# The row of the maxima as four products of 32 rows for two score tiles, and the head's weights' copy and statistics in another order

## The reference

```python
h = group_norm(x)                                   # 32 groups
q, k, v = h Wq + bq, h Wk + bk, h Wv + bv           # 64 channels each
attn = softmax((q . k) * 64 ** -0.5, axis=-1)       # 1024 x 1024 per image
x = x + (attn v) Wo + bo
```

## Time and profile before

| | |
|---|---|
| median of 3 runs | 186.11 us |
| profiled execution | 186.48 us |
| its span on the core | 184.0 us |
| PE busy | 174.6 us (95%), 1223 products |
| DVE busy | 138.3 us (75%) |
| ACT busy | 100.4 us (55%) |
| POOL busy | 121.8 us (66%) |

### The profile page before, as it was taken

One profiled execution on the slowest core, in us unless ns is written; L12 is line 12 of the kernel. 1 busy time (PEld: TensorE's weight loads), 2 busy tenths in 40 slices (PEclk: granted clock), 3 DMA queues, 4 the chain that ended last, 5 costly groups with the idle time before them and its releaser, 6 DMA issues.

```text
span 184.0 us, 3303 instructions
## 1 busy us (share of the span) xinstructions
PE 174.6 (95%) x1223; PEld 93.5 (51%) x1223; DVE 138.3 (75%) x208; ACT 100.4 (55%) x137; POOL 121.8 (66%) x81
## 2 busy tenths in 40 slices
PE   7778899999999999999999999999999999999993
PEld 4435545555525644455535645555535555456661
DVE  2799987779887687859875787769875588386763
ACT  3479367606656376436666476527656554466500
POOL 5265017996799929996699949996799939705000
PEclk9999999999999999999999999999999999999999
DMA  5544100500016000420025000500025100110111
GB/s 154 189 100 98 34 2 0 114 4 2 0 34 142 2 0 14 102 60 0 0 54 122 0 4 20 136 18 0 5 59 115 61 0 21 37 61 7 50 57 57
DMA packets 7103, 8.89 MB, mean 48 GB/s; under 512 B 1656, under 2 KB 4144, under 8 KB 7088
## 3 DMA queue, kind: packets, MB, share of 16 engines
q1 hardware_dynamic: 6080, 7.84, 16.9%
q10 hardware_dynamic: 1008, 0.86, 1.6%
HBM read 1.58 MB, written 1.05 MB: 14 GB/s over the span
## 4 chain that ended last, share of the span: by engine, by line
PE 82%; DVE 13%; DMA 1%; issue 1%; POOL 0%; ACT 0%; DVEq 0%; POOLq 0%
PE ps_attn L887 27%; PE ps_max L817 9%; DVE part_max L588 8%; PE ps_scores L855 8%; PE ps_scores L871 7%; PE ps_scores L857 7%; PE ps_scores L859 7%; PE ps_scores L796 3%; PE ps_misc L804 2%; PE ps_attn L894 2%; PE ps_misc L900 2%; DMA xs<-x_dram 1%; PE ps_misc L894 1%; DVE quarter_rden L628 1%; PE ps_misc L831 1%
## 5 line engine op out<-in xcount | busy, mean ns | idle before, releaser
L313 POOL TENSOR_TENSOR prob_sum<-prob_sum,probs 128x1024 f32<-128x1024 f32 x41 | 97.5, 2377 | 29.0 <-ACT probs L441 16.8
L588 DVE TENSOR_REDUCE part_max<-ps_max 128x2 f32<-128x1024 f32 x60 | 73.4, 1224 | 26.3 <-PE ps_max L818 25.8
L441 ACT ACTIVATE probs<-ps_scores 128x1024 f32<-128x1024 f32 x62 | 61.0, 1025 | 46.1 <-PE ps_scores L872 45.4
L887 PE MATMUL ps_attn<-probs,vals 128*64 128x512 f32 x224 | 54.5, 605 | 0.0
L887 PEld LDWEIGHTS ps_attn<-probs,vals 128*64 128x64 f32 x224 | 13.5, 136 | 27.8 <-issue 19.2
L871 PE MATMUL ps_scores<-q_row,ones_r 64*128 64x512 f32 x62 | 24.5, 396 | 0.5 <-ACT q_row L423 0.5
L872 PE MATMUL ps_scores<-q_row,ones_r 64*128 64x512 f32 x62 | 24.6, 396 | 0.0
L817 PE MATMUL ps_max<-back,front 64*128 64x512 f32 x31 | 13.9, 449 | 2.3 <-DVE part_max L588 1.4
L817 PE MATMUL ps_max<-cross,front 64*128 64x512 f32 x29 | 14.6, 505 | 0.3 <-DVE part_max L588 0.3
L818 PE MATMUL ps_max<-cross,back 64*128 64x512 f32 x29 | 14.6, 505 | 0.0
L818 PE MATMUL ps_max<-front,back 64*128 64x512 f32 x31 | 14.0, 450 | 0.0
(11 more groups left out here) (157 smaller groups left out, 365.7 us busy)
## 6 DMA issues: line engine op xcount, KB each, us to landing
cross<-front SPq DMA_DIRECT2D x16, 128.0 KB, 2.3
cross<-back SPq DMA_DIRECT2D x16, 128.0 KB, 2.3
rden<-quarter_rden SPq DMA_DIRECT2D x44, 32.0 KB, 1.8
xs<-x_dram SPq DMA_DIRECT2D x4, 256.0 KB, 4.6
out_dram<-xs SPq DMA_DIRECT2D x3, 256.0 KB, 2.0
rden<-quarter_rden ACTq DMA_DIRECT2D x12, 32.0 KB, 1.9
q_row<-max_rows SPq DMA_DIRECT2D x14, 2.0 KB
layer<-layers_dram SPq DMA_DIRECT2D x1, 194.5 KB, 2.7
```

Of the source, the lines that this page charges most:

```text
L313: pool.tensor_tensor(total[:, :], total[:, :], probs[t][:, :], ALU.add).then_inc(added, 1)
L441: act.activation(probs[t][:, :], scores_buffer(u, t)[:, :], ACT.Exp, scale=SCALE).then_inc(exp_done, 1)
L588: dve.tensor_reduce(part_max[u % 2][:, at:at + 2 * JS + 1:2 * JS], ps[:, :].rearrange("p (g n) -> p g n", g=2), AX.X, ALU.max, negate=True ...
L887: mm = pe.matmul(ps_attn[half * C:(half + 1) * C, :], v, probs[t][:, cols], start=(t == 0), stop=(t == TILES - 1))
```

## The change

Three things change. For pairs of score tiles a new function `rows_of_pair` adds the row of the maxima to both tiles with four products of 32 rows, on partitions 0 to 31, 32 to 63, 64 to 95 and 96 to 127: left and right half of two tiles. For this SP writes the maxima on four partitions (0, 32, 64, 96), with four transfers a unit in place of two from unit 2 on. Where it is called with `first=True`, its products open the two tiles and `scores_main` closes them; with `first=False` (tiles 0 and 1) they close both. It is used in the loop for all four pairs and in the last unit for tiles (0, 1), (3, 4) and (6, 7). Where `scores_row` stays (units 0 and 1, tiles 2 and 5 of the last unit), it takes its ones from a new matrix `first_r`, which is one on partitions 0 and 64 and zero elsewhere, so that a row that is there twice counts once.

In the head, ACT copies the weights of layer 0 (`copy_setup(0)`), and DVE's `setup` goes. DVE's first step of the statistics of image 1 moves ahead of `affine(0)`.

```diff
             def place_rows(u):
...
-                for n in range(2):
-                    row = q_row[u % 2][n * C:n * C + 1, :].bitcast(F32).rearrange("p (t n) -> p t n", t=JS)
+                for q in (0, 2, 1, 3)[:2 if u == 1 else 4]:
+                    row = q_row[u % 2][q * QUARTER:q * QUARTER + 1, :].bitcast(F32).rearrange("p (t n) -> p t n", t=JS)
+                    n = q // 2
                     sp.dma_start(row, max_rows[n * JS:(n + 1) * JS, :].bitcast(F32)).then_inc(row_in[u % 2], 16)
...
             pool.memset(q_row[1][:, :].bitcast(F32), 0.0).then_inc(rows_zero, 1)
+            pool.memset(first_r[:, :].bitcast(F32), 0.0).then_inc(first_zero, 1)
+            pool.wait_ge(first_zero, 1)
+            for n in range(2):
+                pool.memset(first_r[n * C:n * C + 1, :].bitcast(F32), 1.0).then_inc(first_r_set, 1)
+            pool.wait_ge(first_r_set, 2)
             root(1)
...
             set_back(0)
+            copy_setup(0)
             apply_norm_first()
...
             own_stats(0)
             share_stats(0)
             join_stats(0)
+            own_stats(1)
             affine(0)
             apply_norm_first()
-            setup(0)
-            own_stats(1)
             share_stats(1)
...
-            def scores_main(u, t):
-                front_u, back_u, cross_u = front[u % RING], back[u % RING], cross[u % RING]
+            def scores_ready(u, t):
                 if t == 0:
...
+            def scores_main(u, t, row_first=False):
+                front_u, back_u, cross_u = front[u % RING], back[u % RING], cross[u % RING]
+                if not row_first or t == 0:
+                    scores_ready(u, t)
...
+                if row_first:
+                    mm.then_inc(scores_mm, 1)
...
-                pe.matmul(left, ones_r[top, :], row[top, :], start=False, stop=True)
-                pe.matmul(right, ones_r[low, :], row[low, :], start=False, stop=True).then_inc(scores_mm, 1)
+                pe.matmul(left, first_r[top, :], row[top, :], start=False, stop=True)
+                pe.matmul(right, first_r[low, :], row[low, :], start=False, stop=True).then_inc(scores_mm, 1)
+
+            def rows_of_pair(u, t, first=True):
+                row = q_row[u % 2]
+                if t == 0:
+                    pe.wait_ge(row_in[u % 2], last_row(u))
+                for i in range(2):
+                    if first and (t or i):
+                        scores_ready(u, t + i)
+                    elif first and u:
+                        pe.wait_ge(exp_done, TILES * u - 1)
+                    ps = scores_buffer(u, t + i)
+                    for n, cols in enumerate(halves()):
+                        lanes = quarter(2 * n + i)
+                        mm = pe.matmul(ps[:, cols], ones_r[lanes, :], row[lanes, :], start=first, stop=not first)
+                if not first:
+                    mm.then_inc(scores_mm, 2)
...
                 next_max(2)
-                scores(w, 0)
-                scores(w, 1)
+                scores_main(w, 0)
+                scores_main(w, 1)
+                rows_of_pair(w, 0, False)
                 next_max(3)
...
                 next_max(4)
-                scores(w, 2)
-                scores(w, 3)
+                rows_of_pair(w, 2)
+                scores_main(w, 2, True)
+                scores_main(w, 3, True)
                 next_max(5)
...
                 values(w, 0)
                 if prep:
-                    scores(w, 4)
+                    rows_of_pair(w, 4)
+                    scores_main(w, 4, True)
                     next_max(6)
-                    scores(w, 5)
+                    scores_main(w, 5, True)
                     pe.wait_ge(exp_done, TILES * w + 5)
                     project(w + 2)
...
-                scores(w, 6)
-                scores(w, 7)
+                rows_of_pair(w, 6)
+                scores_main(w, 6, True)
+                scores_main(w, 7, True)
                 next_max(9)
```

More of the change, by code:

```diff
@@ L71, in attention_pair @@
         ones_r = sb("ones_r", [P, P], F32R)
+        first_r = sb("first_r", [P, P], F32R)
         minus_half = sb("minus_half", [P, 1])
@@ L113, in attention_pair @@
         ones_r_set = sem("ones_r_set")
+        first_zero = sem("first_zero")
+        first_r_set = sem("first_r_set")
         half_set = sem("half_set")
@@ L122, in attention_pair @@
         setup_mm = sem("setup_mm")
-        setup_done = sem("setup_done")
         wvo_set = sem("wvo_set")
@@ L183, in last_row @@
         def last_row(unit):
-            return 32 * (unit // 2) if unit % 2 == 0 else 32 * (unit // 2 + 1)
+            return 64 * (unit // 2) if unit % 2 == 0 else 64 * (unit // 2) + 32
         def low_count(later, head, unit):
@@ L410, in bias_x @@
             def bias_x(u):
[L411 to L414, removed]
+                act.wait_ge(wvo_set, u // B + 1)
                 act.wait_ge(h_ready, u + 1)
@@ L628, in reciprocal @@
                 dve.reciprocal(quarter_rden[:, cols], sums).then_inc(quarter_done, 1)
[L630 to L638, removed]
             def pair_tail(u):
@@ L854, in scores_main @@
                 left, right = ps[:, HI], ps[:, LO]
-                pe.matmul(left, key_top[top, hi], front_u[top, HI], start=True, stop=False)
-                pe.matmul(right, key_low[low, hi], back_u[low, HI], start=True, stop=False)
+                pe.matmul(left, key_top[top, hi], front_u[top, HI], start=not row_first, stop=False)
+                pe.matmul(right, key_low[low, hi], back_u[low, HI], start=not row_first, stop=False)
                 pe.matmul(left, key_top[top, hi], front_u[top, LO], start=False, stop=False)
                 pe.matmul(right, key_low[low, hi], back_u[low, LO], start=False, stop=False)
-                pe.matmul(left, key_top[top, lo], front_u[top, HI], start=False, stop=False)
-                pe.matmul(right, key_low[low, lo], back_u[low, HI], start=False, stop=False)
+                pe.matmul(left, key_top[top, lo], front_u[top, HI], start=False, stop=row_first)
+                mm = pe.matmul(right, key_low[low, lo], back_u[low, HI], start=False, stop=row_first)
+                if row_first:
+                    mm.then_inc(scores_mm, 1)
             def scores_row(u, t):
@@ L949, in _ @@
             project(0)
-            pe.wait_ge(setup_done, 1)
+            pe.wait_ge(wvo_set, 1)
             project_v(0)
@@ L981, in _ @@
             scores_main(0, 0)
-            pe.wait_ge(wvo_set, 1)
+            pe.wait_ge(wvo_set, 2)
             pe.wait_ge(max_joined, 1)
@@ L985, in _ @@
             pe.wait_ge(ones_r_set, 1)
+            pe.wait_ge(first_r_set, 2)
             scores_row(0, 0)
@@ L1102, in _ @@
                     project_v(w + 2)
-            scores(LAST, 0)
-            scores(LAST, 1)
+            scores_main(LAST, 0)
+            scores_main(LAST, 1)
+            rows_of_pair(LAST, 0, False)
             scores(LAST, 2)
@@ L1110, in _ @@
             denominators(LAST - 1)
-            scores(LAST, 3)
-            scores(LAST, 4)
+            rows_of_pair(LAST, 3)
+            scores_main(LAST, 3, True)
+            scores_main(LAST, 4, True)
             scores(LAST, 5)
@@ L1116, in _ @@
             values(LAST, 1)
-            scores(LAST, 6)
-            scores(LAST, 7)
+            rows_of_pair(LAST, 6)
+            scores_main(LAST, 6, True)
+            scores_main(LAST, 7, True)
             values(LAST, 2)
```

## The result

| | before | after |
|---|---|---|
| median | 186.04 us (185.86 to 186.34, 4 runs) | 189.9 us (188.72 to 190.46, 4 runs) |
| ratio, 95% interval | | 1.0183 [1.0147, 1.022] |
| profiled execution, span | 186.48, 184.0 us | 188.72, 186.8 us |
| a loop unit (mean of three) | 20.47 us | 21.24 us |

The kernel became slower, as forecast (189.0). The measured median lies 0.1 us above the upper end of the range (184.0 to 189.8); the ratio answers to 189.4 (186.04 x 1.0183).

The account below looks back on a forecast made before the run. PE was taken to bound the kernel (82% of the wait chain). Shape changes and late tiles less saved slots gave +3.3 us, the head -0.44, so +2.9 on the 186.11 median: 189.0 us, range 184.0 to 189.8.

Parts of the forecast that it names:

- The price of a change: On PE, each switch between 64*128 and 32*128 was taken to cost 0.19 us, between bounds of nothing and 0.19.
- The waits in a steady unit: Units w = 2 to 5: late exponentials delay DVE's sum and the projection; +0.37, +0.56 less overlap and +0.15, together +0.71 us each.
- pair (6,7): Last tile pair of a steady unit: two changes of shape against one saved slot, +0.15 us.
- Changes less slots: In w = 6, where DVE has no statistics, changes alone were counted: 7 x 0.19 - 4 x 0.23 = +0.41 us.
- w = 6 and the last unit: Final two units, counted by shape changes less saved slots alone: +0.41 us and +0.07 us.
- The head: Before the loop, DVE's first projection shift at 8.85 instead of 9.29: -0.44 us, bounds -0.87 and nothing.
- The upper bound: Top of the forecast range, 189.8 us, from the head's bounds and 0.02 of doubt on each of 39 changes.
- the sum: Row products +3.3 us over all units; with the head's -0.44, +2.9 us for the whole change.
- Free mixing: Rival: all 39 added shape changes on PE cost nothing, so saved slots win; -2.15 us, 184.0 us, chance 0.28.
- stop without load: Rival: 32-row weights are loaded ahead on PE, a change costs only 0.08; no change, 186.1 us, chance 0.08.
- two by two: Rival: PE's four 32-row products run in twos, each pair loses its slot; 5.3 us more, 194.3 us, chance 0.06.

Follow-up runs that it names:

- rows of 32 at the old places: Kernel before with each row of the maxima multiplied as two products of 32 rows instead of 64, same places and order: 207.22 us.
- Tiles 0 and 1 put back alone: The pairs alone, but with the first two tiles of each unit in the old form: 187.85 us, ratio 1.0085.
- pairs of 64 rows: The pairs alone, same order and waits, but each pair's row as four products of 64 rows in two slots: 188.65 us, ratio 1.0119.
- the pairs alone: Kernel before with only the row products of the change, the head left as before: 190.12 us, ratio 1.0227.
- the copy alone: Kernel before with only the weights' copy moved to ACT, statistics of image 1 in the old order: 185.31 us, again 185.93 (ratios 0.998, 0.9981).

## Why the prediction was right, and where not

- **The price of a change** (0.19, taken between nothing and 0.19): right. The run with rows of 32 at the old places gives 0.17 a change, its rows 0.20. The nested column shapes were the right row to go by. The Trainium skill, page "TensorEngine Tiling (Array Packing)", section Key Properties, says that changing the tiling mode drains TensorE; the trace agrees, with a stop of 0.09 us ahead of the row and 0.17 to 0.20 for the whole change.
- **The waits in a steady unit** (+0.71): measured +0.77. Point by point, with the unit's start shifted by 0.76: DVE's sum forecast at about 106.54, measured 106.56; next maximum 109.25 and 109.28; exponential 4 at 112.69 and 112.73; projection 113.77 and 113.81; pair (6,7) +0.15 and +0.17. The order of the pairs, which completes tiles 0 and 4 later, carries most of it: 0.61 without any change of shape. Tiles 0 and 1 put back alone return 0.40.
- **Waits and changes cover each other.** Changes less slots are 0.41 in every loop unit (7 x 0.19 - 4 x 0.23). Taking them away, as the run with pairs of 64 rows does, gives back only 0.16 in a steady unit (21.24 to 21.08) and 0.18 in w = 6 (17.97 with the pairs alone, 17.79 with pairs of 64 rows, 17.53 before, each from the first score product to that of the next unit). Waits that the order makes anyway come up in their place: the order alone costs 0.61 and 0.26. The prediction had counted it so, by what ends last: waits in a steady unit, changes alone in w = 6.
- **w = 6 and the last unit** (+0.41, +0.07): measured +0.43 and +0.07.
- **The head** (-0.44): this is the step that was mis-sized, in both directions. In the profiled execution it gave 0.79, of which 0.15 is only image 0 landing sooner (3.32 instead of 3.47); on average it gave nothing (1.0024 [0.9996, 1.0052] alone). The mechanism was half right: DVE does start the first projection's shift earlier, but by the copy alone, and the statistics' move makes the gain wait for image 1 (6.19 and 6.95 in two executions, 5.77 to 6.16 without the move). The scatter by PE's rate was not in the prediction at all.
- **The upper bound.** I took the head's bounds and 0.02 on each change. The pairs alone measured +4.2 us [3.5, 5.0] (2.27% of 186), while their profiled execution, the lowest of six, shows +3.4 in the span and +3.6 from the loop on, against the sum's +3.3. The rest is scatter between executions, which one profile can't show; in the pairs alone it is larger than in the run with pairs of 64 rows (188.46 to 188.9). The two longest of the six (190.69 and 191.68) have the lowest granted clock, 0.991 and 0.994 against 0.998 to 1.000; why was not settled.
- **Luck.** The spans of the two profiles differ by 2.8, and the sum was 2.9. Two misses cancel there: the pairs cost 3.6 instead of 3.3, and the head gave 0.79 instead of 0.44. In the medians they don't cancel (+3.9).
- **Rivals.** Free mixing and "stop without load" fell with 0.17 to 0.20 a change; "two by two" fell with 0.43 from the row to the next slot.

## What to carry to other kernels

Before work of two tiles is merged to save an engine's slots, ask which tile is finished later by it and who is waiting for that tile; here the order of the pairs alone cost 0.61 of 0.77 us a unit, and the slots saved did not even pay for the changes of shape. Price a change of PE's array shape at the stop plus the exposed weight load (here 0.08 and 0.11), both ways, by the nearest change that the trace already has. Where two delays end in the same wait they don't add, so take each away by itself before giving either its share.

## What the runs showed of the hardware that was not expected

In the head PE's products can last twice as long while the granted clock reads full: in the first run with the copy alone the view by windows gives 1.00 from 7 to 9 us, where the projection's first product takes 1.02 us to the next one (7.54 to 8.56), 0.53 in the profile of after (7.26 to 7.79):

```profile
7.00:9.00 2.00, 2.00 (x6) 1.00 0.03 10
```

So here the products' own durations, not the clock's row, tell the rate. And a product that had to wait for another engine loses 0.11 us more, though its shape is that of the one before it: the maximum at 110.04 (after) takes 0.43 to the next product, the one at 121.14, which did not wait, 0.32. The weight loads show why: that of the waiting maximum starts with it, that of the other a slot ahead, at 120.92.

```profile
110.04 0.18 PEld L812 LDWEIGHTS ps_max<-cross,front 64*128 64x128 f32 x1 [0.42 <-DVE part_max L594]
...
120.92 0.18 PEld L812 LDWEIGHTS ps_max<-back,front 64*128 64x128 f32 x1
```

So a wait between products of one shape exposes the weight load as a change of shape does.
